# Two graph layers on one core: node products spread over the second pass, another order behind the last chunk

## The reference, cut to what matters

```
h = relu(layernorm(x))
# layer 0
D = |h[:, :, None, :] - h[:, None, :, :]|            # every pair of nodes, 128 channels
s = leaky(batchnorm(D @ W1.T + b1)) @ W2.T + b2      # 64 channels; statistics over all pairs of all graphs
A = softmax(where(adj > 0, s, -9e15))
y = leaky(batchnorm((A @ h) @ Wg.T + bg))            # statistics over all nodes of all graphs
x = x + concat([h, y]) @ Wt.T + bt
# layer 1, with h of the new x
e = where(adj > 0, leaky(hW @ a1 + (hW @ a2).T), -9e15)
x = x + elu(softmax(e, axis=1) @ hW)
```

## Time and profile before

| | us |
|---|---|
| median of 3 runs | 1128.88 (1128.56 to 1129.87) |
| the profiled execution | 1126.25 |
| its span | 1124.3 |
| PE busy | 1049.5 (93%) |
| DVE busy | 1033.1 (92%) |
| ACT busy | 1001.0 (89%) |
| POOL busy | 567.6 (50%) |

### The profile page before, as it was taken

One profiled execution on the slowest core, in us unless ns is written; L12 is line 12 of the kernel. 1 busy time (PEld: TensorE's weight loads), 2 busy tenths in 40 slices (PEclk: granted clock), 3 DMA queues, 4 the chain that ended last, 5 costly groups with the idle time before them and its releaser, 6 DMA issues.

```text
span 1124.3 us, 17526 instructions
## 1 busy us (share of the span) xinstructions
PE 1049.5 (93%) x6390; PEld 461.6 (41%) x6390; DVE 1033.1 (92%) x1381; ACT 1001.0 (89%) x1268; POOL 567.6 (50%) x331
## 2 busy tenths in 40 slices
PE   3899999999999899999999989999999999978997
PEld 1333333333333333333333444233333333357786
DVE  5899999999999999999999985899999999948897
ACT  3889898999999899999999978999999999934897
POOL 5687678778777877777787700111121122201430
PEclk9999999999999999999999999999999999989999
DMA  6345443454444344454444487999999999960012
GB/s 183 139 153 196 159 175 153 168 198 168 194 171 179 140 186 180 168 196 169 185 182 178 179 327 269 337 361 329 334 347 326 342 332 329 324 175 14 20 58 76
DMA packets 99060, 233.31 MB, mean 208 GB/s; under 512 B 9120, under 2 KB 46464, under 8 KB 98976
## 3 DMA queue, kind: packets, MB, share of 16 engines
q1 hardware_dynamic: 86704, 219.97, 53.5%
q0 software_dynamic: 2240, 7.34, 1.8%
q10 hardware_dynamic: 10032, 4.89, 1.7%
HBM read 124.43 MB, written 107.74 MB: 206 GB/s over the span
## 4 chain that ended last, share of the span: by engine, by line
PE 50%; DVE 23%; ACT 14%; issue 9%; POOL 3%; ACTq 1%; DMA 0%; DVEq 0%; POOLq 0%
PE psum L789 21%; PE psum L799 10%; ACT store L674 8%; DVE store L294 8%; PE psum L803 8%; DVE plain_st L1099 3%; PE psum L902 3%; ACT store L593 2%; POOL store L294 1%; PE psum L779 1%; PE psum L761 1%; DVE store L1131 1%; PE psum L877 1%; ACTq L678 1%; DVE bst L1283 1%
## 5 line engine op out<-in xcount | busy, mean ns | idle before, releaser
L294 POOL TENSOR_TENSOR store<-h_ext 128x2048 f32<-128x2048 f32 (+1 forms) x96 | 386.3, 4025 | 95.7 <-PE psum L789 95.7
L789 PE MATMUL psum<-store,w1tt_sb 128*64 128x512 f32 x1792 | 422.8, 598 | 10.9 <-ACT store L593 10.8
L294 DVE TENSOR_TENSOR store<-psum,h_ext 128x2048 f32<-128x2048 f32 x160 | 363.9, 2274 | 0.6 <-ACT h_ext L563 0.6
L593 ACT ACTIVATE store<-store 128x2048 f32<-128x2048 f32 x160 | 305.7, 1928 | 19.3 <-DVE store L294 11.8
L674 ACT ACTIVATE store<-store,st 128x1024 f32<-128x1024 f32 x192 | 227.9, 1240 | 0.0
L789 PEld LDWEIGHTS psum<-store,w1tt_sb 128*64 128x64 f32 x1792 | 122.6, 136 | 249.5 <-issue 214.4
L799 PE MATMUL psum<-store,w_twice 128*64 128x512 f32 x768 | 201.6, 602 | 5.4 <-DVE store L294 2.9
L294 DVE TENSOR_TENSOR store<-h_ext 128x2048 f32<-128x2048 f32 x64 | 146.1, 2283 | 16.3 <-PE psum L789 16.0
L1099 DVE BATCH_NORM_STATS2 plain_st<-store 128x6 f32<-128x512 f32 x256 | 160.5, 678 | 0.0
L803 PE MATMUL psum<-early 128*64 128x512 bf16 x1152 | 159.0, 382 | 0.0
L605 ACT COPY store<-psum 128x1024 f32<-128x1024 f32 x128 | 128.4, 1024 | 16.7 <-PE psum L789 11.6
(11 more groups left out here) (161 smaller groups left out, 1088.4 us busy)
## 6 DMA issues: line engine op xcount, KB each, us to landing
kept_products<-store SPq DMA_DIRECT2D x192, 512.0 KB, 2.9
store<-kept_products SPq DMA_DIRECT2D x192, 512.0 KB, 5.8
early<-score_skew POOLq DMA_DIRECT2D x14, 384.0 KB, 6.8
early<-adj SPq DMA_DIRECT2D x16, 256.0 KB, 3.5
early<-adj_t SPq DMA_DIRECT2D x16, 256.0 KB, 3.6
store<-x ACTq DMA_DIRECT2D x16, 256.0 KB, 5.3
out<-early SPq DMA_DIRECT2D x16, 256.0 KB, 2.3
score_skew<-early POOLq DMA_DIRECT2D x14, 128.0 KB, 6.1
```

The source lines that it names most:

```text
L294: return engine.tensor_tensor(t[:, :, 0:steps, :], nodes.unsqueeze(2).broadcast_to([C, 2, steps, N]), windows(h_ext[:, 2 * c, :], STEP * m ...
L593: nc.scalar.activation(t, t, ACT.Abs).then_inc(abs_ready, 1)
L789: last = nc.tensor.matmul(t[MID * g:MID * g + MID, b, :], w1tt_sb[:, 0:MID], diff[slot][:, g, b * BANK:b * BANK + BANK], start=True, stop= ...
```

## The change

- The fourteen node products of quads 2 to 15 go from the first 21 chunks to one for each quad: PE at n = 16 (u - 2) + 14, ACT's copy at 16 (u - 2) + 17. All but that of quad 1 use bank 4.
- `att_sum` adds -9e15 times the mask (a bf16 tile `none`, made by POOL for each quad, times `neg_ident`) and the turned s_half; DVE's first step adds s_half to it, where it used to add the mask. Loads into s_half wait for that step.
- The third part of the first quad's y_parts is made by DVE at n = 1 instead of by POOL.
- The steps of the last three quads get places of their own (LATE_AT), and the tail has 26 values of n. The last three quads mix in bank 6.
- The loads of x come at n = 257, 262 and 268, eight, four and four, behind the Y and EXP steps due there.
- The output products and folds of x get new places: PRE is 9, AT_END 3, and four are left for layer 1's loop (t = 1 and 2), with waits to match.

```diff
+        LATE_AT = {(NQ - 3, NORM): 253, (NQ - 3, TURN_P): 254, (NQ - 3, COPY): 255, (NQ - 1, EVAC): 257, (NQ - 3, MIX): 257,
+                   (NQ - 3, Y): 257, (NQ - 1, DIST_T): 258, (NQ - 1, TURN): 259, (NQ - 2, SUM): 259, (NQ - 3, Y_SUMS): 260,
+                   (NQ - 2, SCORES): 261, (NQ - 2, EXP): 262, (NQ - 2, NORM): 264, (NQ - 2, TURN_P): 265, (NQ - 2, COPY): 266,
+                   (NQ - 2, MIX): 267, (NQ - 2, Y): 268, (NQ - 1, SUM): 269, (NQ - 2, Y_SUMS): 270, (NQ - 1, SCORES): 271,
+                   (NQ - 1, EXP): 272, (NQ - 1, NORM): 274, (NQ - 1, TURN_P): 275, (NQ - 1, COPY): 276, (NQ - 1, MIX): 277,
+                   (NQ - 1, Y): 278, (NQ - 1, Y_SUMS): 280}
+        LOAD_X = {257: range(0, 8), 262: range(8, 12), 268: range(12, NQ)}
+        def mix_bank(j):
+            return att[0] if j < APART else psum[:, 6, :].rearrange("p (b n) -> p b n", b=QUAD)
...
+        WEIGHED, WEIGHED_OUT = 14, 17
-        def mix_at(n):
-            u, r = divmod(2 * n, 3)
-            return EARLY_MIX + u if r < 2 and 0 <= u < NQ - EARLY_MIX else None
+        def mix_at(n, step):
+            u, r = divmod(n - step, QCH)
+            return EARLY_MIX + u if r == 0 and 0 <= u < NQ - EARLY_MIX else None
...
+        FOLD_AT = (262, 264, 266, 266, 272, 274, 276, 276, 276)
+        MADE_AT = (260, 261, 262, 263, 266, 268, 270, 272, 273)
         PRE = len(FOLD_AT)
         AT_END = 3
-        X_BANK = [j % 4 for j in range(PRE + 1)] + [6, 7, 4, 5]
+        X_BANK = [j % 4 for j in range(PRE + AT_END)] + [4, 5, 7, 6]
...
-            low(0)
...
+            def none_of(j):
+                if j >= 2:
+                    pool.wait_ge(s_sum, j - 1)
+                nc.gpsimd.tensor_scalar(none[:, j % 2, :].rearrange("p (b n) -> p b n", b=QUAD), no_edge[0][:, quad(j), :],
+                                        1.0, None, ALU.mult).then_inc(none_set, 1)
+            nc.gpsimd.tensor_scalar(neg_ident[:, :], ident[:, :], NEG, None, ALU.mult).then_inc(neg_set, 1)
             for j in range(NQ):
+                none_of(j)
...
-                for b in range(QUAD):
-                    nc.tensor.matmul(att[0][:, b, :], ident[:, :], s_half[:, b, 0:N], start=True, stop=False)
-                    last = nc.tensor.matmul(att[0][:, b, :], s_half[:, b, 0:N], ident[:, :], start=False, stop=True)
+                nc.tensor.matmul(att[0], neg_ident[:, :], none[:, j % 2, :], start=True, stop=False)
+                for b in range(QUAD):
+                    last = nc.tensor.matmul(att[0][:, b, :], s_half[:, b, 0:N], ident[:, :], start=False, stop=(b == QUAD - 1))
...
+                if j < APART:
+                    at_zero(QCH * j + MIX)
+                else:
+                    pe.wait_ge(rows_ready, NQ - 1)
+                    pe.wait_ge(weighted_ready, NQ)
+                    if j > APART:
+                        pe.wait_ge(y_out, j)
...
+                if n == 1:
+                    dve.wait_ge(y_mid, 1)
+                    nc.vector.tensor_tensor(y_part(0, 2), by_couple(y_rest[:, :]), y_part(0, 1), ALU.subtract).then_inc(y_split, 1)
...
-                nc.vector.scalar_tensor_tensor(s_shift[:, :, :], no_edge[0][:, quad(j), :], NEG, att[0], ALU.mult, ALU.add)\
+                nc.vector.tensor_tensor(s_shift[:, :, :], att[0], s_half[:, :, 0:N], ALU.add)\
...
-                if t == 1:
-                    for j in range(PRE + AT_END, NQ):
+                if t in (1, 2):
+                    for j in range(PRE + AT_END + 2 * t - 2, PRE + AT_END + 2 * t):
                         fold_x(j)
```

More of the change, by code:

```diff
@@ L704, in _ @@
                         do(j)
+                for q in LOAD_X.get(n, ()):
+                    if q == 0:
+                        act.wait_ge(prod2_ready, NPLAIN)
+                    if q == 8:
+                        act.wait_ge(scored, CHUNKS // 2)
+                    load_x(q)
             def bn_leaky(j):
@@ L977, in turn2 @@
                     pe.wait_ge(h2t_ready, j)
+                else:
+                    pe.wait_ge(x_folded, PRE + 2)
                 for b in range(QUAD):
```

73 lines of the change are left out of this document (41 added, 32 removed).

## The result

| | before | changed | forecast |
|---|---|---|---|
| median of 5 runs, us | 1129.3 (1128.6 to 1131.4) | 1117.1 (1114.6 to 1121.8) | 1112.2 (1105 to 1121) |
| profiled execution, us (span) | 1126.25 (1124.3) | 1117.84 (1115.8) | 1109.5 |
| ratio, 95% interval | | 0.9892 (0.9865 to 0.9919) | |

The kernel became 1.1% faster. The sign and the range held; the size was 4.9 us too favourable by the medians. The last two columns of the budget are a second profile of the same changed kernel, taken with the experiments.

What follows compares the result with a forecast made beforehand. No single engine was taken as the bound: a loop of DVE and ACT set 20.32 us a quad. Terms -1.8 - 11.4 + 5.6 - 10.4 + 1.3 = -16.7 us, from 1128.9 to 1112.2 us, range 1105 to 1121.

Steps and rivals of the forecast that it cites:

- Step 1: Front of the second pass: node products and copies leave the first 21 chunks, net -11.4 us; bounds nothing to -12.3.
- PE's share there fits: Front: PE's 4 score pairs of 1.00 and two products of 1.87 fit in 9.0 us.
- the granted clock: Rival at the front: DMA or PE's clock, staying lower for longer, holds it; half the gain stays, 1118 us; chance 0.13.
- Step 2: Steady part: twelve node copies on ACT inside the loop, +5.6 us, period 20.3 to 20.8; bounds 0 and 13.
- The upper bound (PE in the loop): Steady part: PE's product, not ACT's copy, lies in the loop, 13 us; as a rival 1119.6 us, chance 0.13.
- Step 3: Sum of the scores: PE saves 0.7 us a quad, nothing in the steady part, 0.7 once or twice at the end.
- Step 4: POOL's new neg_ident and none_of (16 x 1.5 us): hidden, 0; 0.4 us a quad kept for the range.
- Step 5: First chunk: low(0) moves from POOL to DVE, shift matmul from 31.62 to 29.8, -1.8 us; bounds 0 and -2.3.
- Step 6: Behind the last chunk: loads of x moved behind the last activation, earlier sums, -10.4 us; bounds -13 and -5.
- Step 7: Layer 1: two more folds on DVE ahead of quad 3's residual, +1.3 us; bounds 0 and +2.2.
- The slower rival: Loop: none_of locks DVE for POOL's 1.49 us in 13 quads, +19.4 us, 1131.6 us; chance 0.06.
- its mark: Sign for none_of locking DVE: L1131 longer than 1.3 us in more than four places.

Runs made afterwards that it cites:

- f4_folds_late: The changed kernel with layer 1's folds of the last two quads at t = 4 instead of t = 2; layer 1 took 99.2 us instead of 100.33.

## Why the prediction was right or wrong

- **Step 1, the front: right way, 8.3 of 11.4 us in the first profile and 10.1 in the second.** No load was waited for, as taken. The step that failed is "PE's share there fits", which priced its pairs at full clock; the cause was named as a rival (the granted clock, as the node products that filled PE are gone), and it took 2.05 us in the first profile and 0.8 in the repeat. The rival's size, half of the gain, was too large. Of the rest, 0.8 us is a none_of (POOL, 709.47 for 4.19) over DVE's last steps for quad 0 (L298 2.82, L1180 1.52).
- **Step 2: right.** 0.49 a quad against 0.46, shown by its removal and by the chain with the copy and without PE. The upper bound (PE in the loop) did not come about at n = 14, but PE held the loop with the product at n = 11 (21.03 to 21.94) and at n = 6 (20.58): the slack was real and narrow. That ACT's idle time "can't" absorb the copy "in a loop that waits at both ends" held for this place of the copy; behind the copy of y half of it was absorbed, until PE's queue with the product was the next bound.
- **Step 3: right.** From SUM(15) to the end of the last sums 9.87 us, against 9.9.
- **Step 4: the value 0 was wrong, the mechanism was in the text.** none_of costs 0.13 to 0.29 in the quads that it meets, some 1.5 us in all, near the low end of the 0.4 a quad kept. The reading of L294 at 841.23 as a sign of no conflict was too weak: 2.27 is its usual length, but there POOL ended 0.47 us behind its start. Where POOL runs on longer, DVE pays: 0.13 us where it ended 1.14 behind (876.71 in the changed kernel), 0.36 where 1.38 behind (832.32 with the copy behind y). The Trainium skill ("SBUF — State Buffer", "Who interferes with whom") was right in direction. Its "for the whole instruction" is not what these rows show: L298 began 0.35 us behind L543 at 876.36, which had 1.14 left, and took 0.13 longer; and L1180 at 836.98 began within an L543 and ended (838.50) ahead of it (838.96). For L1131 at 777.33 the agreement was rough: held until L514's end at 777.89 it would have taken 1.79 us by my working, and it took 1.64.
- **Step 5: -1.3 of -1.8 in the first profile, -2.1 in the second.** Within what twelve profiles scatter (29.48 to 30.31, forecast 29.8). The text lacked that POOL's earlier differences hold L1095 for 1.3 us and PE's first products with it; PE's slack covered that except where its matmuls ran slower.
- **Step 6: -8.8 of -10.4.** Exponentials of quad 14 at 998.0, against 997.8 by the forecast put on this trace (1000.1, less the 2.3 us by which quad 13 is earlier). The term that was mis-sized is the 6.3 us from there to SUM(15): 7.6, as L888 and L987 ran at the lower clock behind PE's wait of 3.23. With the clock at 1.00 behind a wait of 3.19 it was 6.55. In the second profile the tail gained 6.9 only: eight loads took 7.60 to issue and the clock fell again.
- **Step 7: +2.7 of +1.3.** Two folds on the path, 1.2, right, shown by their removal. The other 1.5 is PE's clock, which the sum did not have; it falls without the folds too, and why it did not fall before is open.

The gain missed is 8.2 us between the profiled executions and 4.9 by the medians; that the second is smaller is luck of which executions were profiled. Three shortfalls (front, tail, layer 1) are in large part one omission. Matmuls behind an idle time of PE took up to twice as long for 2 to 4 us, and I priced them by rows at full clock. The slower rival did not come about, though its mark did (13 places for more than four). The mark was badly chosen, as ten of the 13 are beside L537 and outside the loop; and in the loop an instruction is held for 0.1 to 0.4 us here, not for POOL's 1.49.

## What to carry to other kernels

Ahead of each added wait ask what PE's clock does behind it, and give the matmuls there a second price from rows at the lower level, as a bound; fourteen matmuls for nothing before such a place were worth about 1.4 us here in the mean of three profiles. A copy in a loop of two engines can be hidden in the idle time of its engine only on the side where its input is ready, and then the next bound may be the engine that makes the input: here PE, 0.23 us below the old period. Follow the chain of waits before you name the bound; a busy share of 96 to 98% did not make DVE it. Put GpSimd's work where the engine it meets would wait anyway, and judge parts by periods and marks: two profiles of one kernel differed by 2.5 us at the front and 1.9 in the tail, and had the same total.

## What the runs showed of the hardware

- GpSimd and VectorE on SBUF stretch each other by parts: L543 from 1.49 to 4.23 (mean 2.24), L1180 from 1.23 to 1.52 or 1.64, L298 from 2.28 to 2.41 and up to 3.16, L1284 from 0.69 to 0.97. Only the 128x4 L1095 was held to the end of GpSimd's instruction (1.42 for 0.16).
- The issue of eight loads on ACT's queue took 5.91 and 5.68 us before, 6.78 and 7.60 in two executions of the changed kernel, and up to 7.93 in the others; four took 2.05 to 5.36. The exponentials that wait behind them scatter by as much.
- The length of PE's idle time alone did not decide whether the granted clock fell. In layer 1 it fell behind 2.68 us (f4_folds_late, from about 1033.3, with the idle time over at 1031.9) as behind 3.90 (changed kernel, 1035.6), and stayed at 1.00 behind 2.69 before. In the tail it fell behind 3.23 (changed kernel) and stayed at 1.00 behind 3.19 (e4_pe_warm).
